# A Hyena layer in one block of engine programs: input products by rows of 128, the class rows masked, the convolution started behind the last input product

## The reference, cut to what matters

```
u = jnp.einsum('bld,ed->ble', inputs, w_in) + b_in          # 576 rows: x0, x1 and v, 192 each
u = jnp.transpose(u, (0, 2, 1))
up = jnp.pad(u, ((0, 0), (0, 0), (2, 0)))
uc = w_sf[:, 0:1] * up[:, :, 0:L] + w_sf[:, 1:2] * up[:, :, 1:L + 1] + w_sf[:, 2:3] * up[:, :, 2:L + 2] + b_sf[:, None]
uc = uc.reshape(B, N, 3 * HC, L)
x0, x1, v = uc[:, :, 0:HC, :], uc[:, :, HC:2 * HC, :], uc[:, :, 2 * HC:3 * HC, :]
kv = jnp.einsum('bnil,bnjl->bijnl', x1, v)
...                                                         # hkv: causal convolution of kv with h along l
qhkv = jnp.einsum('bijnl,bnil->blnj', hkv, x0)
...                                                         # norm, times w_out, plus b_out, plus inputs
```

## Time and profile before

| | us |
|---|---|
| three executions | 713.42, 713.63, 721.0 |
| median | 713.63 |
| the profiled execution | 713.7 |
| its span in the trace | 711.9 |
| TensorE / VectorE / ScalarE / GpSimd busy | 610.4 / 281.2 / 201.9 / 144.1 |
| the input block's first transpose starts | 497.0 |
| the mix block's first DMA is issued | 540.63 |
| the pair loop's first matmul starts | 546.33 |

### The profile page before, as it was taken

How to read it: one execution, slowest core, us unless ns; L and a number is a source line. 1 busy time by engine, 2 the same in 40 slices (tenths; PEclk the granted TensorE clock), 3 DMA queues, 4 the chain that set the end, 5 groups by cost and what they waited for, 6 DMA issues and landing times. The chain is left out here.

```text
span 711.9 us, 11066 instructions
## 1 busy us (share of the span) xinstructions
PE 610.4 (86%) x4365; PEld 439.2 (62%) x4365; DVE 281.2 (40%) x654; ACT 201.9 (28%) x481; POOL 144.1 (20%) x216
## 2 busy tenths in 40 slices
PE   2023979999999989878999999998987999989996
PEld 1002649555555544335899999988444556749995
DVE  0000042567767558794233333364462215302221
ACT  2001241154444424332533344400340001212220
POOL 6771110011111112332000000001006411232222
PEclk9999999999999999999999999999898999999998
DMA  7406141000000000602977776000722683166650
GB/s 210 157 5 271 63 117 51 1 1 1 2 1 1 2 0 1 161 19 79 359 273 276 290 298 268 1 1 7 270 77 56 237 336 168 35 222 192 184 181 1
DMA packets 27499, 86.75 MB, mean 122 GB/s; under 512 B 7822, under 2 KB 17351, under 8 KB 22330
## 3 DMA queue, kind: packets, MB, share of 16 engines
q1 hardware_dynamic: 24778, 82.89, 33.7%
q0 software_dynamic: 2672, 3.17, 1.7%
HBM read 79.68 MB, written 7.04 MB: 122 GB/s over the span
## 5 line engine op out<-in xcount | busy, mean ns | idle before, releaser
L1556 DVE TENSOR_TENSOR eo<-banks,soft_factors 32x192 f32<-32x192 f32 x128 | 45.3, 354 | 91.8 <-PE banks L1506 71.0
L1537 ACT ACTIVATE ex<-banks,soft_b 128x128 f32<-128x128 f32 x192 | 51.2, 398 | 73.4 <-PE banks L1492 73.4
L889 DVE TENSOR_REDUCE nm<-banks 128x1 f32<-128x453 f32 x96 | 55.9, 623 | 31.6 <-PE banks L662 31.3
L1506 PE MATMUL banks<-soft_pair_w,ex 128*128 128x192 f32 x384 | 66.4, 330 | 1.6 <-issue 1.6
L680 PE MATMUL banks<-qa,kt 32*99 32x256 f32 (+1 forms) x384 | 65.9, 399 | 0.0
L849 ACT ACTIVATE pt<-banks 128x1024 f32<-128x1024 f32 (+1 forms) x48 | 49.1, 1023 | 57.2 <-PE banks L680 57.2
L662 PE MATMUL banks<-kt,qt 32*128 32x453 f32 x192 | 62.5, 590 | 2.3 <-DVE nm L889 0.9
L1506 PEld LDWEIGHTS banks<-soft_pair_w,ex 128*128 128x128 f32 x384 | 62.0, 190 | 3.4 <-issue 1.7
L1487 PE MATMUL banks<-slots_a,soft_pair_w 128*128 128x128 f32 x384 | 45.9, 276 | 1.2 <-PEq L1256 1.1
L1487 PEld LDWEIGHTS banks<-slots_a,soft_pair_w 128*128 128x128 f32 x384 | 44.9, 192 | 2.3 <-issue 2.0
L84 PE MATMUL banks<-dense 128*128 128x512 bf16 x151 | 40.5, 409 | 4.7 <-PEq L2537 4.1
(11 more groups left out here) (292 smaller groups left out, 1015.9 us busy)
## 6 DMA issues: line engine op xcount, KB each, us to landing
soft_pair_w<-in_spair SPq DMA_DIRECT2D x32, 1152.0 KB, 7.5
hy_band<-in_hband SPq DMA_DIRECT2D x6, 1540.0 KB, 6.6
route_tile_wi<-in_wi SPq DMA_DIRECT2D x15, 576.0 KB
switch_wo<-in_wo SPq DMA_DIRECT2D x1, 4608.0 KB, 16.1
hy_x_spread<-x_rows SPq DMA_DIRECT2D x24, 128.5 KB, 5.2
sorted_x<-blank_rows SPq DMA_DIRECT2D x15, 193.0 KB
route_tile_x<-sorted_x SPq DMA_DIRECT2D x15, 193.0 KB
vt<-in_vt SPq DMA_DIRECT2D x1, 2496.0 KB
```

The source lines that it names most:

```text
L889: dve.tensor_reduce(nm[:, n % 2, j, at:at + 1], ps[:, q, 0:NK], AXX, ALU.max, negate=True).then_inc(maxed, 1)
L1506: mm = pe.matmul(ps[:, 6 + q, 0:D], hid[:, p % 2, q, j, :], w[:, at:at + D], start=j == 0, stop=j == HJ - 1)
L1537: ins = act.activation(hid[:, p % 2, q, j, :], hidden(p, q, j), ACT.Gelu, bias=k.b1[:, 2 * p + q, j:j + 1])
L1556: dve.tensor_tensor(eo[SL * r:SL * (r + 1), b, i, :], ps[SL * b:SL * (b + 1), 6 + e % 2, 0:D], b2[SL * r:SL * (r + 1), i, :], ALU.add).the ...
```

## The change

The two blocks become one. `hyena_inputs` becomes a class `Inputs` whose methods are called from the engine lists of the mix block.

- The products are of 128 rows: first 128 rows of x0 (`W_X0`), then three of 64 rows of x1 over 64 rows of v (`W_FIRST` to `W_FIRST + 2`), then the last 64 rows of x0 (`W_X0_REST`), whose images 0, 1 and 2, 3 lie on the two halves of the rows. The turned x1 and v of one third of the heads come out of one `turn` (8 transposes) and four copies of ScalarE.
- The class rows are multiplied by a mask on VectorE (`mask_cls`), gathered by a single matmul per third (`pick_cls`), and spread by VectorE (`cls_outer`).
- Small tables are joined: `taps` and `consts` (667 KB) take the place of ten DMAs. `win`, `u`, `uc` and `u0` lie in the buffer of the switch experts' weights, which are loaded later.
- Both `keep_busy` trains (4 and 14 matmuls) are gone.
- The pair loop stands directly behind `turn` and `pick_cls` of the second third; those of the last third are called behind the loop's first two pairs.
- GpSimd starts `outer` once the first third's x1 and v are copied.

```diff
...
+    def sync(self, sp, a):
+        x = self.x
+        sp.dma_start(x.taps[:, :], a["htaps"]).then_inc(x.taps_in, 16)
+        first = DC * P
+        sp.dma_start(x.win[:, 0:first], a["hwin"][:, 0:first]).then_inc(x.taps_in, 16)
+        sp.dma_start(x.win[:, first:], a["hwin"][:, first:]).then_inc(x.win_in, 16)
+        sp.dma_start(x.consts[:, :], a["hconsts"]).then_inc(x.const_in, 16)
+        for g in range(2):
+            x.load_band(sp, a, g)
+        sp.dma_start(x.wout[:, :, :], a["hwout"]).then_inc(x.wout_in, 16)
+        sp.dma_start(x.bout[:, :], a["hbout"].broadcast_to([P, D])).then_inc(x.wout_in, 16)
+        sp.wait_ge(x.c2, W_X0 + 1)
+        sp.dma_start(x.x0d[0:P], x.u0).then_inc(x.x0_out, 16)
+        sp.wait_ge(x.x0_out, 16)
+        for g in range(2):
+            x.load_x0(sp, g)
+        sp.wait_ge(x.c2, W_X0_REST + 1)
+        for u in range(2):
+            sp.dma_start(x.x0d[P:D, 2 * u:2 * u + 2, :], x.u0_rest[u * HALF:(u + 1) * HALF, :, :]
+                         ).then_inc(x.x0_rest_out, 16)
...
+    def product(self, pe, q):
+        bank, w = 2 * (q % 2), HALF if q == W_X0_REST else P
...
+        if q == W_X0:
+            pe.wait_ge(x.taps_in, 32)
+        if q == W_FIRST:
+            pe.wait_ge(x.win_in, 16)
+        if q >= 2:
+            pe.wait_ge(x.ur, 3 * (q - 1))
+        if q == W_X0_REST:
+            for d in range(DC):
+                for u in range(2):
+                    mm = pe.matmul(ps[u * HALF:(u + 1) * HALF, bank, 0:512], weight[d],
+                                   k.xt[0:DK, d, u * 512:(u + 1) * 512], start=d == 0, stop=d == DC - 1)
+            mm.then_inc(x.um, 2)
+            pe.wait_ge(x.ur, 3 * q)
+            for d in range(DC):
+                for u in range(2):
+                    lo = TAIL * P + 2 * u * QUAD
+                    mm = pe.matmul(ps[u * HALF:(u + 1) * HALF, 4, 0:2], weight[d],
+                                   k.xt[0:DK, d, lo:lo + 2 * QUAD:QUAD], start=d == 0, stop=d == DC - 1)
...
+    def turn(self, pe, n):
+        k, x = self.k, self.x
+        pe.wait_ge(x.c2, W_FIRST + n + 1)
+        if n >= 1:
+            pe.wait_ge(x.xr, 4 * n)
+        for j in range(JT):
+            for b in range(B):
+                mm = pe.transpose(k.ps[:, 6 + j, b * P:(b + 1) * P], x.uc[:, n, b, 1 + j * P:1 + (j + 1) * P],
+                                  k.ident[:, :])
+        mm.then_inc(x.tm, 1)
+    def pick_cls(self, pe, n):
+        x = self.x
+        pe.wait_ge(x.mask_r, n + 1)
+        if n >= 1:
+            pe.wait_ge(x.cls_r, n)
+        pe.matmul(self.k.ps[:, 5, 0:2 * CH * B], x.pick[:, n, :], x.masked[:, n, :], start=True, stop=True
+                  ).then_inc(x.cls_m, 1)
...
+    def copy_turned(self, act, n):
+        x = self.x
+        part = slice(n * HALF * B, (n + 1) * HALF * B)
+        act.wait_ge(x.tm, n + 1)
+        for j in range(JT):
+            src = self.k.ps[:, 6 + j, 0:512].rearrange("p (b t n i) -> p b t n i", b=B, t=2, i=CH)
+            for t, (dst, order) in enumerate(((x.x1, "p (n i b) -> p b n i"), (x.v, "p (n b i) -> p b n i"))):
+                act.activation(dst[:, j, part].rearrange(order, b=B, i=CH), src[:, :, t, :, :], ACT.Copy
+                               ).then_inc(x.xr, 1)
...
+    def convolve_taps(self, dve, q):
+        dve.wait_ge(x.ur, 3 * q + 3)
+        dve.tensor_scalar(o, x.u[:, q % 2, 0:n, 0:L], self.tap(q, 0), self.tap(q, 3), ALU.mult, ALU.add
+                          ).then_inc(x.c0, 1)
...
+    def mask_cls(self, dve, n):
+        x = self.x
+        dve.wait_ge(x.c2, W_FIRST + n + 1)
+        dve.tensor_tensor(x.masked[:, n, :].rearrange("p (t b) -> p t b", b=B), bc(x.uc[:, n, :, 0], 1, 2 * CH),
+                          bc(x.taps[:, TAPC - 2 * CH:TAPC], 2, B), ALU.mult).then_inc(x.mask_r, 1)
+    def cls_outer(self, dve, n):
+        ps, x = self.k.ps, self.x
+        half = CH * B
+        dve.wait_ge(x.cls_m, n + 1)
+        dve.tensor_copy(x.cls[:, n, :], ps[:, 5, 0:2 * half]).then_inc(x.cls_r, 1)
+        dve.wait_ge(x.cls_r, n + 1)
+        dve.tensor_tensor(x.kvc[:, n, :].rearrange("p (i b j) -> p i b j", i=CH, b=B),
+                          bc(x.cls[:, n, 0:half].rearrange("p (i b) -> p i b", i=CH), 3, CH),
+                          bc(x.cls[:, n, half:2 * half].rearrange("p (j b) -> p b j", j=CH), 1, CH),
+                          ALU.mult).then_inc(x.kvc_r, 1)
+        dve.wait_ge(x.kvc_r, n + 1)
+        dve.wait_ge(x.const_in, 16)
+        dve.tensor_tensor(x.kvz[:, 2 * n:2 * n + 2, :, :], bc(x.own[:, 2 * n:2 * n + 2, :], 3, KC),
+                          bc(bc(x.kvc[:, n, :], 1, 2), 1, 2), ALU.mult).then_inc(x.kvz_r, 1)
...
                 for g in range(NG):
+                    if g % 2 == 0:
+                        pool.wait_ge(x.xr, 4 * (g // 2 + 1))
...
                 def cls_source(m):
                     c, g = m // GP_, m % GP_
+                    if m % (2 * GP_) == 0:
+                        pe.wait_ge(x.kvz_r, m // (2 * GP_) + 1)
...
-                pe.wait_ge(x.const_in, 48)
-                pe.wait_ge(x.band_in[0], 16)
-                keep_busy(k, pe, MS, 14)
-                pe.wait_ge(w_in, 80)
-                pe.wait_ge(kvz_r, 1)
-                pe.wait_ge(zeroed, 1)
+                turn_rows(k, pe, x.x_turned)
+                inputs.product(pe, W_X0)
+                inputs.product(pe, W_FIRST)
+                inputs.product(pe, W_FIRST + 1)
+                pe.wait_ge(x.const_in, 16)
+                inputs.turn(pe, 0)
+                inputs.product(pe, W_FIRST + 2)
+                inputs.pick_cls(pe, 0)
+                inputs.product(pe, W_X0_REST)
+                inputs.turn(pe, 1)
+                inputs.pick_cls(pe, 1)
+                pe.wait_ge(x.ur, 15)
                 for m in range(0, PAIRS, 2):
                     cls_source(m)
                     cls_source(m + 1)
@@ -1960,6 +2003,9 @@
                         sum_y(m - 2)
                         sum_y(m - 1)
                     convolve(m + 1)
+                    if m == 0:
+                        inputs.turn(pe, 2)
+                        inputs.pick_cls(pe, 2)
...
-                act.wait_ge(w_in, 80)
+                copy_turned(k, act, x.x_turned, x.xt_ready)
+                act.wait_ge(x.pad, 1)
+                act.wait_ge(x.taps_in, 32)
+                inputs.bias(act, W_X0)
+                inputs.bias(act, W_FIRST)
+                inputs.bias(act, W_FIRST + 1)
+                inputs.copy_turned(act, 0)
+                inputs.bias(act, W_FIRST + 2)
+                inputs.bias(act, W_X0_REST)
+                inputs.copy_turned(act, 1)
+                inputs.copy_turned(act, 2)
+                act.wait_ge(x.const_in, 16)
...
-                dve.wait_ge(kvc_r, 1)
-                dve.tensor_tensor(kvz[:, :, :, :], bc(x.own[:, :, :], 3, KC),
-                                  bc(bc(kvc[:, :], 1, 2), 1, NG), ALU.mult).then_inc(kvz_r, 1)
+                dve.wait_ge(x.taps_in, 32)
+                dve.wait_ge(x.pad, 1)
+                inputs.convolve_taps(dve, W_X0)
+                inputs.convolve_taps(dve, W_FIRST)
+                inputs.mask_cls(dve, 0)
+                inputs.convolve_taps(dve, W_FIRST + 1)
+                inputs.mask_cls(dve, 1)
+                inputs.convolve_taps(dve, W_FIRST + 2)
+                inputs.mask_cls(dve, 2)
+                inputs.cls_outer(dve, 0)
+                inputs.convolve_taps(dve, W_X0_REST)
+                inputs.cls_outer(dve, 1)
+                inputs.cls_outer(dve, 2)
...
```

More of the change, by code:

```diff
@@ L1638, in __init__, with part @@
-        self.own = sb("own_pair", [P, NG, 2])
-        self.sel = sb("sel", [P, GP_, P])
+        consts = sb("consts", [P, MIXC])
+        at = [0]
+        def part(n):
+            at[0] += n
+            return consts[:, at[0] - n:at[0]]
+        self.consts = consts
+        self.sel = part(GP_ * P).rearrange("p (g q) -> p g q", g=GP_)
+        self.pick = part(3 * P).rearrange("p (k q) -> p k q", k=3)
+        self.tail = part(P)
+        self.hrow = part(L)
+        self.own = part(2 * NG).rearrange("p (c u) -> p c u", c=NG)
@@ new lines, in __init__ @@
+        self.nw = part(NG)
+        self.image = part(B)
+        self.taps = sb("taps", [P, TAPC])
+        self.wout = sb("w_out", [P, NG, D])
+        self.bout = sb("b_out", [P, D])
+        flat = k.wo[:, :, :, :].rearrange("p e j n -> p (e j n)")
+        self.win = flat[0:DK, 0:DC * 3 * D]
+        lo = DC * 3 * D
+        self.u = flat[:, lo:lo + 2 * B * (L + 2)].rearrange("p (r b l) -> p r b l", r=2, b=B)
+        lo += 2 * B * (L + 2)
+        self.uc = flat[:, lo:lo + 3 * B * L].rearrange("p (k b l) -> p k b l", k=3, b=B)
@@ L1829, in sb @@
             return k.sb(name, shape, dt, st)
+        x = Mixer(k, st)
+        inputs = Inputs(k, x)
         tiles = Tiles(k, out, st)
         kv = sb("hy_kv", [P, 2, JT, HG * KC])
-        kvc = sb("hy_kv_cls", [P, KC])
-        kvz = sb("hy_kv_own", [P, NG, 2, KC])
```

(11 more changed lines are left out.)

280 lines of the change are left out of this document (100 added, 180 removed).

## The result

The changed kernel takes 706.67 us (median of 6 runs, 705.92 to 708.13). With three more runs beside it, the kernel before has a median of 717.63 (713.42 to 721.0). The ratio is 0.985, 95% interval 0.982 to 0.989. It is faster, by 7.7 to 13.2 us; 706.67 lies just above the range's end of 706.5, and 6.7 above the forecast.

What follows compares the result with a forecast made beforehand. TensorE's pair loop, never waiting once started, was taken as the bound. Loop start 529.25 against 546.33 gave −17.1, plus 1.15 for turn and pick and 2.25 for clock: −13.7, from 713.7 to 700.0 us; range 692.5 to 706.5.

Steps and rivals of the forecast that it cites:

- VectorE's waits at 0.875 each, the middle: Ahead of the loop: six VectorE instructions beside GpSimd each lose 0.875 us, 5.25 us in all, loop starting at 529.25.
- rival 2: Ahead of the loop, VectorE waits for whole GpSimd instructions; loop starts at 534.2, −8.7 us, 705.0 us; chance 0.20.
- Everything behind it unchanged in length: Behind the pair loop: all later stretches keep their length, while the loop ends some 13.7 us earlier.
- The start: First product ahead of the loop: starts at 500.9 in place of 503.25, partly at 1.2 GHz, ends at 505.6.
- The products: Ahead of the loop: four products of 3.82 us each and a half product of 1.9, its halves side by side.
- Turn and pick in the loop: The last third's turn (0.9) and pick matmul (0.23) behind the loop's first two pairs add 1.15 us.
- The clock: The loop's first 3.4 to 6.9 us run at half clock, a loss of 1.7 to 3.4 us, taken as 2.25.
- rival 4: Without keep-busy trains the loop does not come back to 2.4 GHz; slower than before, 721 us; chance 0.03.
- Moved DMAs: Loads and stores moved around the loop arrive in time: no cost, some 0.5 us if SyncE is late.
- Rival 1: GpSimd gives way and VectorE isn't held ahead of the loop; loop starts at 524.0, −19.5 us, 694.2; chance 0.20.
- rival 3: The loop waits for something later than `kvz`, such as late x0; about −5 us, 708.5 us; chance 0.07.

Runs made afterwards that it cites:

- split sums: Changed kernel with GpSimd's two long sums over k.h cut into 18 of one tile each; ratio 0.977 to the kernel before.
- fill experiment: Changed kernel with 84 keep-busy matmuls in place of 78 in the train ahead of the first tile; ratio 0.984 to the kernel before.
- the sums late: Changed kernel with GpSimd's two sums moved behind the third group, inside the pair loop; ratio 0.972 to the kernel before.

## Why the prediction came out as it did

- **VectorE's waits at 0.875 each, the middle: wrong, 5.25 us for 8.6.** This is the step of the path to the loop that failed. From the start of the last taps to the loop I had 9.95 us (4.7 of work, 5.25 of waits), and it was 13.30. By the rows after against the undisturbed durations, the waits are 0.1, 0.7, 0.7, 3.5 and 3.6, together 8.6. The mechanism of rival 2 is the right one, as the split sums show: each waits for the rest of the other engine's instruction. What I held against it, the stretched partner of L2009, was the same rule seen from the other side: the outer product behind VectorE's waits in its turn, as the first sum does here (4.80 for 3.85). By that reading L2009 waits for the `outer` to end, near 542.2, and ends at 543.2; it ended at 543.0. A mean over two mechanisms is a third one, for which nothing spoke. The Trainium skill's page "SBUF — State Buffer", section "SBUF: two separate sides", which has the lock held for the whole instruction, agrees with the mask at 3.69 beside a sum of 3.85 and at 0.46 beside pieces.
- **Rival 2's own sum, 705.0, was also off, both ways.** It put the loop 37.25 us behind the stage's first DMA, and it was 34.43: the waits were 8.6 for 10.2, and the taps began 1.2 sooner than I had them. It kept everything behind the loop as it was. It lies nearest to 706.67, in part by luck: its loop starts 2.8 too late, and the 3.8 behind the loop is missing. The range's end is off too: rival 2 with the larger clock loss (3.4 for 2.25) is 706.1 by the forecast's own terms, not 706.5.
- **"Everything behind it unchanged in length": wrong, a term put at nothing that was 3.8 us.** From the first scatter to the first tile load 1.25 longer, and the first tile at 1.2 GHz: 2.5. The fill experiment shows the second for its profile, and 0.8 us of it in the medians. Why the scatters land later isn't shown: both profiles of before have 13.7 or 13.8 there, and every other has 14.3 to 15.4, also the one that only moves table loads and keeps before's order.
- **The start: right in kind.** The half clock at the start lasted until 4.1 us behind the stage's first DMA, and I had 5.7, as before. The first product ended 7.1 us behind the stage's first DMA, and I had 8.65. The fourth ended 20.4 behind it, for 21.45.
- **The products: right.** 3.9 us from one to the next for 3.82, and the half product 1.94 for 1.9, its halves side by side.
- **Turn and pick in the loop: right.** 1.17 for 1.15, and neither the first gate nor the second made TensorE wait.
- **The clock: right.** 3.84 us at half clock, a loss of 1.8 for 2.25, in the forecast 1.7 to 3.4; full clock thereafter, so rival 4 is out.
- **Moved DMAs: right.** No wait in the loop for a band, an x0 row or a table.

By stretches: the loop starts 2.1 later than forecast against the stage, the loop is 0.4 shorter, 3.8 are lost behind it, and 1.8 is the chance of the stages ahead. That makes 7.3 us, the 6.4 of the profiles against 13.7. The measured gain of 11.0 is larger than the profiles' 6.4 since the profiled execution of before was one of its short ones: 713.7 lies 3.9 below the median of its six runs, and the one after, 707.24, 0.6 above its own. The forecast of 700.0 stands on that short execution; its gain of 13.7 is 2.7 from the measured 11.0. That it is so near is partly luck: in the two pairs of profiles the two stretches to the end of the loop shrank by 12.0 and 17.1 us, and the stretches behind it, which I had unchanged, grew by 3.8 and 4.3. Rival 1 is refuted, and rival 3 too: the release is `kv_own`, as said.

## What to carry to other kernels

Before moving work of VectorE beside work of GpSimd, list the length of each GpSimd instruction that it will meet: a 0.2 us instruction on the critical path can cost 3.7, and cutting or moving the long one bought most of that back with no work removed (here 4.4 and 5.8 us of the stage). Where a trace allows two mechanisms, forecast one of them; the middle is neither. A fixed number of keep-busy matmuls is tuned to the latency around it, so look at each such train behind the change, however far, for a wait that has grown. And a shorter approach to a dense loop isn't all gain: two of the shortened ones gave back 1.4 and 1.9 us of it, mostly in a longer stretch at 1.2 GHz.

## What was unexpected of the hardware

- `tensor_scalar` with one SBUF tensor of 1028 fp32 elements is held beside GpSimd as well: 1.60 us for 0.81, and 0.81 for 0.54 on 514 elements beside the split sums. `scalar_tensor_tensor` of the same length beside one of the long sums took 4.75 for 1.29.
- Waiting is mutual and alternates: beside a chain of 1.1 us outer products each two-input tap waits 0.72, and GpSimd's four then take 6.56 us, for 1.10 each undisturbed.
- A single wait of 4.13 us more among light work made the loop's first 10 us run at 1.2 GHz, where the changed kernel's cost 3.84 us of it. But less waiting is not always less: with the sums late TensorE waits 2.74 and 0.38 us in place of 6.23 and 3.72, and the loop ran at 1.2 GHz for about 6.6 us.
- The kernel before took 49.38 and 54.49 us for the same stretch in two executions. The stretch has light work in four places, and 3.8 us of the difference lie in work at a low clock beside them.
